# Value tiles of a new batch made in three slots of the first head, and split by GpSimd in its last slot

## The reference

```python
Q = proj(Wq); K = proj(Wk); V = proj(Wv)                      # per head: Q1, Q2, K1, K2, V
A1 = einsum('bhqd,bhkd->bhqk', Q1, K1) * scaling
A2 = einsum('bhqd,bhkd->bhqk', Q2, K2) * scaling
attn = softmax(A1, axis=-1) - lam * softmax(A2, axis=-1)
O = einsum('bhqk,bhkd->bhqd', attn, V)
O = O / sqrt(mean(O * O, axis=-1, keepdims=True) + EPS) * rms_scale * (1.0 - LAMBDA_INIT)
x = x + einsum('bne,de->bnd', O, Wo)
```

## Time and profile before

| | |
|---|---|
| median of 3 runs | 2924.59 us (2921.78 to 2926.59) |
| profiled execution | 2920.77 us, its span 2919.0 us |
| TensorE busy | 2749.3 us (94%) |
| VectorE busy | 2376.8 us (81%) |
| ScalarE busy | 1997.8 us (68%) |
| GpSimd busy | 1041.8 us (36%) |
| value tiles, L134 | 32 instructions, 340 ns at the median, 4 groups of 8 |

### The profile page before, as it was taken

How to read it: one execution, slowest core, us unless ns; L and a number is a source line. 1 busy time by engine, 2 the same in 40 slices (tenths; PEclk the granted TensorE clock), 3 DMA queues, 4 the chain that set the end, 5 groups by cost and what they waited for, 6 DMA issues and landing times.

```text
span 2919.0 us, 43834 instructions
## 1 busy us (share of the span) xinstructions
PE 2749.3 (94%) x14770; PEld 1818.2 (62%) x14770; DVE 2376.8 (81%) x3982; ACT 1997.8 (68%) x3998; POOL 1041.8 (36%) x1558
## 2 busy tenths in 40 slices
PE   4799999999889999899999999999999999999996
PEld 2122222222278888677777777777777777777774
DVE  7999999999355555677777888888888888888887
ACT  5388888888742233477777777777777777777772
POOL 4200000000010000155555565555655556565561
PEclk8699999999989999999999999999999999999997
DMA  2220000000010000000000000000000000000000
GB/s 76 77 80 23 13 23 23 23 13 12 1 59 1 1 1 1 1 1 1 1 1 1 1 1 1 1 1 1 8 1 1 1 1 8 1 1 1 1 1 15
DMA packets 31023, 34.98 MB, mean 12 GB/s; under 512 B 7656, under 2 KB 18896, under 8 KB 30672
## 3 DMA queue, kind: packets, MB, share of 16 engines
q1 hardware_dynamic: 30800, 32.18, 3.8%
HBM read 23.37 MB, written 8.39 MB: 11 GB/s over the span
## 4 chain that ended last, share of the span: by engine, by line
PE 49%; DVE 6%; issue 1%; POOL 1%; ACT 1%; POOLq 0%; DVEq 0%; ACTq 0%
PE ps L1609 7%; PE ps L1610 7%; PE ps L1550 7%; PE ps L1612 7%; PE ps L1538 7%; DVE neg_maxima L1815 2%; PE ps L1566 2%; PE ps L1568 1%; PE ps L1567 1%; PE ps L1556 1%; PE ps L1555 1%; PE ps L1554 1%; PE ps L1527 1%; PE ps L1528 1%; PE ps L1529 1%
## 5 line engine op out<-in xcount | busy, mean ns | idle before, releaser
L1815 DVE TENSOR_REDUCE neg_maxima<-ps 128x1 f32<-128x1024 f32 x512 | 624.7, 1220 | 148.2 <-PE ps L1612 144.0
L656 ACT ACTIVATE probs<-ps 128x512 f32<-128x512 f32 x1024 | 535.2, 606 | 172.2 <-PE ps L719 172.0
L1758 ACT ACTIVATE diff_probs<-ps,neg_maxima 128x1024 f32<-128x1024 f32 x512 | 575.9, 1125 | 88.1 <-DVE neg_maxima L1815 86.4
L572 DVE TENSOR_REDUCE maxima_of_halves<-ps 128x2 f32<-128x1024 f32 x512 | 602.5, 1220 | 17.1 <-PE ps L676 12.6
L1609 PE MATMUL ps<-z_T_high,y_high 128*128 128x512 f32 x1024 | 465.3, 454 | 6.6 <-ACT diff_probs L1758 5.2
L2080 POOL TENSOR_TENSOR DT_low<-DT_whole,DT_high 128x512 fp32r<-128x512 f32 x256 | 334.7, 1308 | 351.9 <-DVEq L1983 309.2
L1610 PE MATMUL ps<-z_T_low,y_high 128*128 128x512 f32 x1024 | 404.6, 395 | 0.0
L1827 DVE SCALAR_TENSOR_TENSOR D<-diff_probs,ratio 128x1024 f32<-128x1024 f32 x256 | 336.1, 1313 | 9.4 <-DVE ratio L1823 0.4
L719 PE MATMUL ps<-q_stacks,k_stacks 51*128 51x512 bf16 x1024 | 314.2, 386 | 20.5 <-ACT probs L656 14.6
L1612 PE MATMUL ps<-z_T_high,y_low 128*128 128x512 f32 x1024 | 319.3, 393 | 0.0
L1538 PE MATMUL ps<-identity,D 128*128 128x128 f32 x2048 | 307.2, 273 | 1.7 <-ACT arena L1700 1.7
(11 more groups left out here) (300 smaller groups left out, 4998.6 us busy)
## 6 DMA issues: line engine op xcount, KB each, us to landing
q_stacks<-q_parts_dram SPq DMA_DIRECT2D x192, 32.0 KB
q_parts_dram<-qk_parts SPq DMA_DIRECT2D x12, 256.0 KB, 2.4
k_parts_dram<-qk_parts SPq DMA_DIRECT2D x12, 256.0 KB, 3.4
k_stacks<-k_parts_dram SPq DMA_DIRECT2D x32, 96.0 KB
residual<-in_L_attn_x_dram SPq DMA_DIRECT2D x4, 512.0 KB, 6.2
k_stacks<-k_parts_dram SPq DMA_DIRECT2D x32, 64.0 KB
q_stacks<-neg_max_parts SPq DMA_DIRECT2D x96, 4.0 KB, 1.7
out_dram<-residual SPq DMA_DIRECT2D x3, 512.0 KB, 3.2
```

Source lines behind the costliest of these rows:

```text
L572: nc.vector.tensor_reduce(mx_half[:, own, half, :, p * PB + t, :], ps[:, bank:bank + 2, :], X, ALU.max).then_inc(nat_max, 1)
L656: nc.scalar.activation(probs[:, k % PT, h, :], ps[:, (r + k + i) % S_RING, :], ACT.Exp, scale=SCALE).then_inc(s_free, 1)
L1758: nc.scalar.activation(probs[:, t % 2, m, :], ps[:, 2 * m:2 * m + 2, :].rearrange("p k n -> p (k n)"), ACT.Exp, bias=neg[:, t, m:m + 1], a ...
L1815: nc.vector.tensor_reduce(neg[:, t, m:m + 1], ps[:, 2 * m:2 * m + 2, :].rearrange("p k n -> p (k n)"), X, ALU.max, negate=True).then_inc(m ...
```

## The change

`take_z` of VectorE takes the tiles it makes (`first`, `n`) and is called three times: for two tiles of `z`, for the other two, and for the four of `z_rest`; in slots 1, 2 and 3 of head 0 and in slots 4, 5 and 6 of heads 8, 16 and 24, now ahead of the slot's FP4 steps and behind `add`. `z_ready` counts three steps for a batch in place of one: TensorE's part 0 waits for the second, GpSimd for the third. GpSimd's `take_z` moves from slot 4 to the last slot (7) of these three heads, behind `low_DT` and `weight`; in head 0 it stays in slot 4.

```diff
@@ pe.slot
-                                pe.wait_ge(z_ready, own[0] + 1)
+                                pe.wait_ge(z_ready, own[0] * 3 + 2)
                             else:
                                 pe.wait_ge(z_split, own[0] * 2 + 2)
@@ dve
-                def take_z(b):
-
-                    for t in range(PB):
+                def take_z(b, first, n):
+
+                    for t in range(first, first + n):
                         to = z[:, t, :] if t < HALF else z_rest[:, t - HALF, :]
                         ins = norm_tile(norm, dve, to, core.x, b * PB + t)
                     ins.then_inc(z_ready, 1)
@@ dve.slot
                     if t == 1 and not last:
-                        take_z(0)
+                        take_z(0, 0, 2)
+                    if t == 2 and not last:
+                        take_z(0, 2, 2)
+                    if t == 3 and not last:
+                        take_z(0, HALF, HALF)
...
                     if last:
                         add(n - PB, t, last[0])
+                    if last and begins_batch(last, own):
+                        if t == G:
+                            dve.wait_ge(u_psum, it * 2 + UP0)
+                            take_z(own[0], 0, 2)
+                        if t == G + 1:
+                            take_z(own[0], 2, 2)
+                        if t == G + 2:
+                            take_z(own[0], HALF, HALF)
                     fp4_steps(it, t, starts, ends)
...
-                    if t == G and last and begins_batch(last, own):
-                        dve.wait_ge(u_psum, it * 2 + UP0)
-                        take_z(own[0])
@@ pool
-                    wait_first(pool, z_ready, b + 1)
+                    wait_first(pool, z_ready, b * 3 + 3)
...
-                    if t == G and begins_batch(last, own):
+                    if t == (PB - 1 if last else G) and begins_batch(last, own):
                         take_z(own[0])
```

## The result

Over 20 runs of each the kernel went from 2921.74 us (2918.92 to 2926.62) to 2927.73 us (2922.97 to 2934.25): ratio 1.0018, 95% interval [1.0012, 1.0024], so 3.5 to 7.0 us slower. The forecast was +7.4 us, just above that interval, and a time of 2932.0 us, 4.3 above the median of the 20 runs: 2.9 of these come from its base, the median of three runs (2924.59), which lies that much above the median of twenty. The measured ratio is also under the forecast's own line of 0.2% for "slower", so it counts as "same" there, to which it gave 35%.

A forecast was written before the change was run, and what follows sets the result against it. Batch beginnings cost 10.56 us over ordinary heads, all the change could win. 3 x (4.2 wait + 1.9 clock) = 18.3, less 10.56, with head 0's -0.3: +7.4 us on 2924.59, 2932.0 us; range about 2924.6 to 2937.

The forecast's parts named there:

- The wait in slot 7: Heads 8, 16, 24: TensorE waits 4.0 us for GpSimd's late split; 3.7 to 4.6 us more from slot 4 to slot 0.
- the held pair of slot 5: Slot 5's two value tiles stand behind GpSimd's WG_head, 0 to 1.0 us; slot 7 then some 0.9 us later, half taken.
- The clock: After TensorE's wait its clock falls to about half; price 1.9 us a batch, from 1.6 up to about 3.
- The 1.6 us read from head 8: Kernel before: head 8's stretch less head 16's, 30.56 - 28.97 us, taken as the price of the clock's fall.
- The rival without a fall: The clock stays at 1.00 despite the 4 us wait: +0.2 to +2.9 us, 2926 us; chance 22%.
- The rival of +11.6 us: Half rate lasts 6.9 us and the pair is blocked each time: 2936 us and a little over; chance 12%.
- The three beginnings: Heads 8, 16, 24 cost 18.3 us over ordinary heads, less the 10.56 they cost before: +7.7 us.
- Head 0: Tiles in slots 1, 2, 3 in place of 1: -0.3 us, between 0 and -1; the split may block D.
- the pair's term: Half of the extra 0.9 us if slot 5's pair is blocked, raising the stretch's 3.7 us to 4.2 a batch.
- Slots 4 and 6: Two tiles make slot 5 0.55 us late; slot 6's four tiles take 1.1 us against 1.02 us of VectorE slack.
- The faster rival: GpSimd's split is ready 4 us sooner, so TensorE doesn't wait for it in slot 7: -9.4 us, 2915 us; chance 6%.

The follow-up runs named there:

- e2: Changed kernel plus 15 unread matmuls on TensorE ahead of its wait for the split in heads 8, 16, 24; ratio 1.0000 to the kernel before.
- e6: e1 with the value tiles of head 0 made in slot 1 again, as in the kernel before; ratio 0.9989 to the kernel before.
- e1: Changed kernel with GpSimd's split in slot 6 in place of slot 7 of heads 8, 16, 24; ratio 0.9994 to the kernel before.
- e8: e6 with slot 5's pair of value tiles moved into slot 4: four tiles there, four in slot 6; ratio 0.9974 to the kernel before.
- e3: Kernel before with only GpSimd's split moved from slot 4 to slot 6 of heads 8, 16, 24; ratio 1.0003 to the kernel before.
- e5: Changed kernel without GpSimd's WG_head work in slot 5 of heads 8, 16, 24 (stale weights); one execution, slot 4 to slot 0 31.96, 30.93, 31.10 us.
- e4: Kernel before with only GpSimd's split moved from slot 4 to slot 7 of heads 8, 16, 24; ratio 1.0050 to the kernel before.
- e7: Changed kernel with GpSimd's split still in slot 7 but ahead of DT_low and the weight steps; ratio 1.0009 to the kernel before.

## Why the prediction was right

The mechanism was right: the wait, what made it, its length and the fall of the clock. That the sum came so close in the profile is partly luck, as the terms below show.

**The wait in slot 7** (forecast 4.0 us, 3.7 to 4.6 in the stretch) is 3.48 to 3.68 us, and 3.5 to 3.7 in the stretch by e2. The chain that made it was worked out from an ordinary head step by step, and each step is in the rows above. I had allowed half of a further 0.9 us for the held pair of slot 5. The pair was held by 0.7 us in all three heads, yet slot 7 began only 0.7 us late (0.5 in head 8), about the 0.5 that was laid out without the hold: slot 5 took 0.44 us more than an ordinary one and slot 6 a little less. So in head 16 the split ended within 0.2 us of where the working without the hold had it, and by this term the sum was 0.6 us a batch too high. TensorE came to its wait 0.5 us late, which makes the wait shorter than the 4.0 and leaves the stretch as it is.

**The clock** (forecast 1.9 us, between 1.6 and 2.9) was worth 2.53, 1.33 and 2.33, 2.06 in the mean. The mean hides two lengths, 6.8 us at half rate in two heads and 3.4 in one. The 1.6 us read from head 8 were not the clock alone: TensorE's wait there was 0.66 us longer than in head 16 (2.18 for 1.52) before the clock fell. The rival without a fall was wrong in all three heads. The rival of +11.6 us had its conditions largely met, the pair held each time and the long fall in two heads of three. Its prices were too high: the hold cost the stretch next to nothing (0.9 in the rival), a long fall 2.3 to 2.5 us (2.9).

**The three beginnings** came to 95.0 us against 77.9 for ordinary ones: 17.1 where I had 18.3, less the 10.56 that they cost before: +6.5 for +7.7.

**Head 0** had the wrong sign: -0.3 forecast, +0.7 measured (e6). The step that failed is the one that looked for contention only between the split and D; the tiles themselves stood behind DT_low, twice. This error of +1.0 and the +0.5 by which the clock was under-sized cancel most of the 1.7 us that the pair's term was too high: +7.2 in the profile for +7.4. Over the 20 runs the difference was smaller, 5.3 us by the ratio and 6.0 by the medians; whether the clock fell for less time in those executions than in the profiled one no trace shows.

**Slots 4 and 6** went about as laid out: slot 4 took 0.36 us more than an ordinary one (forecast 0.55), and the four tiles of slot 6 fitted in VectorE's slack.

**The faster rival** wanted the split 4 us earlier. e1 shows what it would take, one slot sooner, and that even then not all is won.

The Trainium skill (SBUF — State Buffer, "Who interferes with whom") gave the held pair by rule: a tensor_scalar in a two-port mode and a GpSimd instruction exclude each other. The rows agree for 128 x 128 tiles (1.29 for 0.59 us) and for one of 8 columns in e1 (1.01 for 0.17); in which mode they ran no row shows.

## What to carry to other kernels

A producer that is moved later must be timed against its consumer through the whole list of the engine that does it: here the split stood behind five other GpSimd instructions, one of them itself held, and 3.7 us of in-order wait on the busiest engine ate all that the spreading gave. When a wait falls on TensorE, count the low clock that comes with it too; it was 6.2 of the 17.1 us that the three beginnings cost. Spreading VectorE work over slots pays where GpSimd is idle beside it: four tiles in one slot where it was idle (e8) beat two and two. And a semaphore mark that stands alone in an engine's queue doesn't say that the work before it is done; here it let GpSimd start early, beside the tiles that it then held (e3, e5).

## What the runs showed of the hardware

The same wait can leave the clock alone or not. In e1 TensorE waited 1.97 us in head 16 and in head 24; behind the first the clock stayed at 1.00, behind the second it fell, as the windows around the two show:

```profile
2055.00:2072.00 17.00, 15.03 (x70) 1.00 0.11 33
...
2482.00:2490.00 8.00, 8.00 (x34) 0.79 0.01 3
```

Over all ten profiles, TensorE's waits in the heads that begin a batch go as follows. Those of 1.30 to 1.54 us (before, e1, e6, e8) had no fall in six of six; those of 1.93 to 1.97 (e1, e3, e4, e6) had one in six of eight; those of 2.17 and 2.18 (before, e3, e4) in three of three; those of 2.4 us and over (the changed kernel, e4, e5, e7) in twelve of twelve.

How much an instruction loses beside GpSimd's does not depend on how small it is: a ratio step of one column took 1.07 us in e3 for 0.22, and ended at 2050.83, with the GpSimd instruction beside it (2050.82). What counts is what is left of that instruction.
